# Splitting the last stage's weights during attention, 256 columns per pair, with both parts waiting in DRAM

## The reference

```python
xn = layernorm(x)
qu, ku, vu, qc, kc, vc = split(xn @ W_qkv.T)          # 8 heads of 64 each
term1     = causal(qc * s @ vu.T)                     # s = 64 ** -0.5
lookahead = causal(sigmoid(qu * s @ ku.T))
Su        = term1 @ lookahead.T
scores    = qc * s @ kc.T - silu(Su)                  # masked above the diagonal
attn_out  = (softmax(scores) @ vc) @ W_out.T
h         = silu(xn @ (w_gate / 127).T) * (xn @ (w_up / 127).T)
out       = x + attn_out + h @ (w_down / 127).T
```

## Time and profile before

| what | value |
|---|---|
| median of 3 runs | 1144.9 us |
| profiled execution, own time | 1145.91 us |
| profiled execution, span of its instructions | 1144.2 us |
| PE busy | 1092.3 us (95% of the span) |
| DVE, ACT, POOL busy | 815.2, 763.5, 534.2 us (71%, 67%, 47%) |
| DMA | 73.22 MB, mean 64 GB/s |
| mean granted TensorE clock | 0.988 of full |

### The profile page before, as it was taken

One profiled execution on the slowest core, in us unless ns is written; L12 is line 12 of the kernel. 1 busy time (PEld: TensorE's weight loads), 2 busy tenths in 40 slices (PEclk: granted clock), 3 DMA queues, 4 the chain that ended last, 5 costly groups with the idle time before them and its releaser, 6 DMA issues.

```text
span 1144.2 us, 21233 instructions
## 1 busy us (share of the span) xinstructions
PE 1092.3 (95%) x7936; PEld 992.5 (87%) x7936; DVE 815.2 (71%) x1671; ACT 763.5 (67%) x1371; POOL 534.2 (47%) x623
## 2 busy tenths in 40 slices
PE   5899999999999999999999999999999859999997
PEld 4799999999898899998999899999999757888997
DVE  5577677777777777777777777777667777567665
ACT  4577777777777777777777777777777846344333
POOL 0255556455645564555455555555555554231130
PEclk9999999999999999999999999999999969999999
DMA  8000201020002000200020012001100403745641
GB/s 284 1 2 19 75 22 22 17 77 22 22 17 76 24 25 13 80 21 20 17 76 20 19 24 70 20 19 39 37 20 19 157 19 130 274 149 176 224 152 57
DMA packets 36952, 73.22 MB, mean 64 GB/s; under 512 B 2288, under 2 KB 15856, under 8 KB 34800
## 3 DMA queue, kind: packets, MB, share of 16 engines
q1 hardware_dynamic: 36848, 71.84, 20.0%
HBM read 42.47 MB, written 32.24 MB: 65 GB/s over the span
## 4 chain that ended last, share of the span: by engine, by line
PE 87%; DVE 7%; issue 2%; ACT 1%; DMA 1%; DVEq 0%; POOL 0%; SPq 0%; ACTq 0%
PE X L637 23%; PE X L561 20%; PE X L675 8%; PE X L752 7%; PE X L743 6%; PE X L591 6%; PE X L646 6%; PE X L605 4%; PE X L576 4%; DVE prob L1147 3%; PE X L621 2%; DMA v_s<-heads_out 1%; PE X L552 1%; DVE low_max L1106 0%; DVE L_s L1200 0%
## 5 line engine op out<-in xcount | busy, mean ns | idle before, releaser
L637 PE MATMUL X<-L_s,T_s 128*128 128x128 f32 (+3 forms) x1920 | 278.9, 303 | 10.0 <-DVE L_s L1119 10.0
L487 POOL TENSOR_SCALAR prob<-prob,inv 128x512 f32<-128x512 f32 (+3 forms) x256 | 278.0, 1103 | 17.1 <-DVE inv L1159 17.1
L637 PEld LDWEIGHTS X<-L_s,T_s 128*128 128x128 f32 x1920 | 267.0, 191 | 20.5 <-issue 10.1
L561 PE MATMUL X<-xT,W 128*128 128x512 f32 x960 | 237.5, 400 | 8.5 <-DVE least L1147 7.0
L561 PEld LDWEIGHTS X<-xT,W 128*128 128x128 f32 x960 | 178.8, 191 | 50.4 <-DVE least L1147 9.7
L900 ACT ACTIVATE gate<-X 128x1024 f32<-128x1024 f32 (+1 forms) x96 | 84.8, 883 | 130.1 <-PE X L637 130.1
L1147 DVE CUSTOM_DVE_ANT_0 prob<-X,gate 128x512 f32<-128x512 f32 (+3 forms) x256 | 109.9, 485 | 73.8 <-PE X L621 73.7
L1133 DVE SCALAR_TENSOR_TENSOR gate<-gate,X 128x1024 f32<-128x1024 f32 (+1 forms) x96 | 99.6, 1038 | 77.9 <-ACT gate L900 77.9
L908 ACT ACTIVATE prob<-prob,least 128x512 f32<-128x512 f32 (+3 forms) x256 | 141.2, 562 | 8.5 <-DVE least L1147 8.5
L477 POOL TENSOR_SCALAR_AFFINE_SELECT T_s<-T_s 128x512 fp32r<-128x512 f32 x128 | 111.1, 889 | 67.0 <-DVE T_s L1126 67.0
L469 POOL TENSOR_SCALAR_AFFINE_SELECT tanh_l<-tanh_l 128x256 f32<-128x256 f32 (+1 forms) x96 | 46.2, 497 | 205.6 <-ACT tanh_l L878 205.6
(11 more groups left out here) (82 smaller groups left out, 1816.3 us busy)
## 6 DMA issues: line engine op xcount, KB each, us to landing
heads_out<-o_s SPq DMA_DIRECT2D x64, 256.0 KB, 3.3
xT_copy<-xT SPq DMA_DIRECT2D x8, 1024.0 KB, 7.6
xb<-in_L_attn_x SPq DMA_DIRECT2D x8, 512.0 KB, 5.8
xT<-xT_copy SPq DMA_DIRECT2D x4, 1024.0 KB, 5.2
tanh_l<-in_L_attn_x SPq DMA_DIRECT2D x8, 512.0 KB, 5.4
gate<-heads_out SPq DMA_DIRECT2D x4, 1024.0 KB, 8.0
T_s<-heads_out SPq DMA_DIRECT2D x4, 1024.0 KB, 9.7
L_s<-xT_copy SPq DMA_DIRECT2D x4, 1024.0 KB, 6.2
```

The source lines that it names most:

```text
L487: last = pool.tensor_scalar(v, v, inv[:, h, w - 1:w], None, ALU.mult)
L561: last = pe.matmul(out, sh.W[:, a, k, cols], xT[:, c, k, :], start=(n == 0), stop=(n == 3 * KD - 1))
L637: last = pe.matmul(both[:, h, at:at + (J + 1) * P], T_s[:, h, a, to:to + P], L_s[:, h, c, WIDE[J + 1]:WIDE[J + 1] + (J + 1) * P], start=(J ...
```

## The change

The four weights, 22 chunks of 128 x 256 (18 of integers, 4 of W_out), are now loaded, split and stored one chunk a step, in steps 4 to 25. SP's step stores the two parts of the last chunk and loads the next raw one; ACT copies a chunk to its high part; DVE subtracts and, for integer chunks, takes the largest low part. The flag is made piece by piece in steps 22 to 25. The DRAM tensors `w_split` hold both parts, so step 31 loads twice the bytes and splits nothing. The early DRAM copies are gone, and so is SP's wait for the maxima ahead of the load of the attention output. PE waits for the loads instead of the subtractions. In `ffn_first` ACT now does the second group of exp of pair 31 ahead of `copy_o`.

```diff
+CHUNK = 256
+INT_CHUNKS = 3 * KD * HIDDEN // CHUNK
+CHUNKS = INT_CHUNKS + OT * DIM // CHUNK
+FIRST_CHUNK = 4
...
             def step(part, b, q, g, back1, back2, ahead):     # SP
+                c = g - FIRST_CHUNK
+                if 1 <= c <= CHUNKS:
+                    store_chunk(c - 1)
+                if 0 <= c < CHUNKS:
+                    load_chunk(c)
+                if c == INT_CHUNKS + 1:
+                    sp.wait_ge(low_most_taken, 1)
+                    sp.dma_start(low_row[:, :], low_most[:, :]).then_inc(low_max_gathered, 16)
...
                     load_xT(0)
+                    sp.wait_ge(chunk_stored, CHUNKS * 16)
                     for n in range(4):
-                        sp.wait_ge(w_copied[n], 16)
-                        sp.dma_start(placed[n][:, LOW, :].bitcast(F32 if n == 3 else I32), w_copy[n]).then_inc(w_loaded[n], 16)
+                        sp.dma_start(placed[n].bitcast(F32), w_split[n]).then_inc(w_loaded[n], 16)
...
+            def load_chunk(c):
+                n, at = chunk_of(c)
+                src = (w_gate, w_up, w_down, W_out)[n]
+                r, d = at // src.shape[1] * P, at % src.shape[1]
+                to = w_raw[:, :].bitcast(F32) if n == 3 else w_raw[:, :]
+                sp.dma_start(to, src[r:r + P, d:d + CHUNK]).then_inc(chunk_loaded, 16)
+            def store_chunk(c):
+                n, at = chunk_of(c)
+                sp.wait_ge(w_low, c + 1)
+                sp.sem_inc(ticks, 1)
+                sp.dma_start(w_split[n][:, :, at:at + CHUNK], w_parts[:, :, :].bitcast(F32)).then_inc(chunk_stored, 16)
...
-            copy_weights()
...
             load_xres(0)
-            sp.wait_ge(low_max_taken, 3)
-            sp.dma_start(low_row[:, :], low_max[:, :]).then_inc(low_max_gathered, 16)
             sp.wait_ge(scores_emptied, after(LAST_G, 2))
             load_o(0)
...
             def ffn_first(products):                          # PE
-                pe.wait_ge(w_low, 2)
+                pe.wait_ge(w_loaded[0], 16)
+                pe.wait_ge(w_loaded[1], 16)
...
+            def high_chunk(c):                                # ACT
+                act.wait_ge(chunk_loaded, c * 16 + 16)
+                if c > 0:
+                    act.wait_ge(chunk_stored, c * 16)
+                raw = w_raw[:, :].bitcast(F32) if chunk_of(c)[0] == 3 else w_raw[:, :]
+                act.activation(w_parts[:, HIGH, :], raw, ACT.Copy).then_inc(w_high, 1)
...
                 exp_of(LAST_G, 0)
+                exp_of(LAST_G, 1)
                 copy_o(LAST_G - 1, double[3])
-                exp_of(LAST_G, 1)
...
+            def low_chunk(c):                                 # DVE
+                dve.wait_ge(w_high, c + 1)
+                raw = w_raw[:, :].bitcast(F32) if chunk_of(c)[0] == 3 else w_raw[:, :]
+                dve.tensor_tensor(w_parts[:, LOW, :], raw, w_parts[:, HIGH, :].bitcast(F32), ALU.subtract) \
+                   .then_inc(w_low, 1)
...
                 low_L(g, 2)
-                if part == LAST and q == 3:
-                    low_weights(2)
+                if 0 <= g - FIRST_CHUNK < CHUNKS:
+                    low_chunk(g - FIRST_CHUNK)
                 if ahead:
                     low_proj(g + 1, VU, par)
...
                     low_values(g + 2, (q + 1) // 2 % 2, (q + 1) % 2)
+                if 0 <= g - FIRST_CHUNK < INT_CHUNKS:
+                    take_low_max(g - FIRST_CHUNK)
```

More of the change, by code:

```diff
@@ L170, with layer @@
 BEFORE = bank_history()
-def layer(nc, x, W_qkv, w_gate, w_up, w_down, W_out, w_copy, xT_copy, sh, heads_out, out):
+def layer(nc, x, W_qkv, w_gate, w_up, w_down, W_out, w_split, xT_copy, sh, heads_out, out):
     ctx = ExitStack()
@@ L273, in layer @@
         w_loaded = [sem(f"w_loaded{i}") for i in range(4)]
-        w_copied = [sem(f"w_copied{i}") for i in range(4)]
+        chunk_loaded = sem("chunk_loaded")
+        chunk_stored = sem("chunk_stored")
         low_max_taken = sem("low_max_taken")
+        low_most_taken = sem("low_most_taken")
         low_max_gathered = sem("low_max_gathered")
@@ L1032, in step @@
                     exp_of(g - 1, 0)
-                if part == LAST and q == 3:
-                    high_weights(1)
                 if ahead:
@@ L1039, in step @@
                 high_L(g, 2)
-                if part == LAST and q == 3:
-                    high_weights(2)
                 if ahead:
@@ L1045, in step @@
                     high_xT(part, b)
-                if part == LAST and q == 3:
-                    high_weights(3)
                 if ahead:
@@ L1222, in ffn_first @@
                 minus_scores(LAST_G, 2, double[1])
-                take_has_low()
                 inverse(LAST_G, 1)
@@ L1296, in step @@
                     minus_scores(g - 1, 2)
-                if part == LAST and q == 3:
-                    low_weights(0)
                 if ahead:
                     low_proj(g + 1, QU, par)
-                if part == LAST and q == 3:
-                    low_weights(1)
-                if ahead:
                     low_proj(g + 1, KU, par)
@@ L1313, in step @@
                     ln.scale(dve, b + 1)
-                if part == LAST and q == 3:
-                    low_weights(3)
                 if ahead:
                     low_values(g + 2, (q + 1) // 2 % 2, (q + 1) % 2)
+                if 0 <= g - FIRST_CHUNK < INT_CHUNKS:
+                    take_low_max(g - FIRST_CHUNK)
+                if g - FIRST_CHUNK >= INT_CHUNKS:
+                    take_has_low(g - FIRST_CHUNK)
                 if back1:
@@ L1330, in step @@
                     low_PT(g - 1, 0)
-                if part == LAST and q == 3:
-                    take_low_max(0)
-                    take_low_max(1)
-                    take_low_max(2)
                 silu_of(g, 2)
@@ L1363, in build @@
         sh = Shared(nc, ctx)
-        layer(nc, x_rows, W_qkv, w_gate, w_up, w_down, W_out, w_copy, xT_copy, sh, heads_out, out_rows)
+        layer(nc, x_rows, W_qkv, w_gate, w_up, w_down, W_out, w_split, xT_copy, sh, heads_out, out_rows)
 _INS = ["L0_attn_x", "L0_attn_W_qkv", "L0_attn_W_out", "L0_ffn_w_gate", "L0_ffn_w_up", "L0_ffn_w_down"]
```

52 lines of the change are left out of this document (25 added, 27 removed).

## The result

The changed kernel takes **1133.6 us** (median of 6 runs, 1131.33 to 1135.83). The kernel before, run beside it, takes 1144.9 (6 runs, 1143.78 to 1145.54). The ratio is 0.9903, with a 95% interval of 0.9889 to 0.9916: about 1% faster. The forecast was 1132.7, range 1129.5 to 1137.5. The profiled execution was the slowest of the six: own time 1135.83, span 1134.0 us, against 1145.91 and 1144.2. Two single executions of about twice the usual time, one of the kernel before (2061 us, beside the runs on the chunks) and one of warm_start (2104 us), are left out of all that follows.

A forecast was written before the change was run, and what follows sets the result against it. The prediction took PE to set the pace, with two long idle waits around step 31. Its terms, 3.7 + 5.0 + 2.8 + 0.7 = 12.2 us, took the median of 1144.9 to 1132.7 us, range 1129.5 to 1137.5.

The forecast's parts named there:

- What bounds the kernel: Steady attention: PE sets the pace; around step 31 it idles 9.96 us ahead of `sum_up` and 6.18 ahead of `drain`.
- Term 1: Ahead of `sum_up` of step 31: splitting removed, PE's wait shrinks from 9.96 to 6.2 us, -3.7 us; clock still falls.
- Term 2: Ahead of `drain`: DVE's three reductions removed, PE's wait falls from 6.18 to 1.1 us, -5.0 us.
- Term 3: Scores and attend of `drain`: after a short wait the clock stays full, 4.96 us instead of 7.80, -2.8 us.
- Term 4: `ffn_first`: with ACT's exp done earlier, the third gate product comes 4.6 us after attend instead of 5.34, -0.7 us.
- Term 5: The 22 steps that get chunk work: hidden under idle time of ACT and DVE, 0 us; 27 us if none were hidden.
- Term 6: SP and DMA: the extra chunk transfers and step 31's doubled weight load stay hidden, the latter by 25 us; 0 us.
- The sum: Whole kernel: 3.7 + 5.0 + 2.8 + 0.7 = 12.2 us, all on PE's path, giving 1132.7 us.
- Rival A: Chunk steps: POOL's norm blocks DVE's subtractions, costing 2 to 6 us, 1135 to 1139 us; chance 0.10.
- Rival B: Last stage: POOL's additions slow DVE, PE waits, clock falls again, 4 to 5 us come back, 1137 us; chance 0.08.
- Rival C: Every chunk step: ACT or DVE late for `sum_up`, slower than before, up to 15 us over, 1160 us; chance 0.03.
- Rival D: Ahead of `drain`: ACT's gate, not DVE's reductions, set the wait; terms 2 and 3 nil, 1140.5 us; chance 0.05.

The follow-up runs named there:

- warm_start: Changed kernel plus unused matmuls and transposes in PE's waits at the start, meant to remove the start's scatter; 1135.5 us.
- subtract2: Changed kernel with two DVE operations of 128x1536 put back ahead of the last L_s of step 31, without ACT's copies; 1135.9 us.
- warm31: Changed kernel with 24 unused matmuls on PE in the 6.2 us wait ahead of `sum_up` of step 31; 1130.3 us.
- reduce3: Changed kernel with three reductions of 1536 columns put back on DVE ahead of the last gate of step 31; 1139.9 us.
- order_only: Kernel before with only ACT's order changed: second group of exp of pair 31 ahead of `copy_o`; 1144.5 us, ratio 0.9994.
- chunk3: Changed kernel with each chunk's copy, subtraction and reduction done three times, at the change's place; 1137.9 us.
- flag_late: Changed kernel with the last two flag operations moved back to `ffn_first`, behind the last row minima; 1137.1 us.
- chain1: Changed kernel with each chunk's copy and subtraction, once each, moved into the chain ahead of the step's last L_s; 1133.5 us.
- chain3: Changed kernel with chunk copy and subtraction moved ahead of the step's last L_s, and every chunk operation done three times; 1169.9 us, ratio 1.0198.
- reduce1: Changed kernel with one reduction of 1536 columns put back on DVE ahead of the last gate of step 31; 1137.8 us.
- again: The changed kernel itself, unedited, run and profiled once more; 1133.7 us.

## Why the prediction was right, step by step

- **What bounds the kernel** held: only the two long waits and what follows them moved, and steps 3 to 31 take as long as before to 0.2 us.
- **Term 1** was right to 0.05 us, with its reason: DVE's queue brings the wait back by itself (subtract2), and by the rows ACT's high part would have been next. That the clock would fall all the same was right too: 0.50 behind 6.21 us of waiting. The "up to 3 us more" of a clock that holds were 2.4 on the 48 matmuls, and 3.3 on the medians, when warm31 made it hold.
- **Term 2** was right to 0.02 us (reduce3 gives it back).
- **Term 3** was right in size (-3.08 against -2.8), and its cause was half of it. The prediction read the 7.80 us of `drain` as a slow clock alone. In that profile the clock was indeed low to the end of attend, but where it comes up sooner, the kernel before needs 7.81 all the same, for the flag (order_only), and only with the early flag 6.18 (reduce3). So by these two runs 1.5 of the 3.1 us come from the shorter wait, and the other 1.6 from the early flag. The right size was luck: it was read from one profile in which the clock stayed low for 6.4 us behind the restart, as long as the flag held PE. In order_only, behind the same wait, it was up after some 3 us and PE then stood idle for 1.51 us: a reader of that profile would have seen that the clock is only a part of the 7.80.
- **Term 4** was right on the timeline (4.77 us; forecast 4.6). Alone it brings 0.65 us on the timeline and between the medians, too little for the runs to show it (order_only).
- **Term 5**, 22 chunk steps at no cost, was right: 798.3 and 798.1 us, the same 28 waits of 6.4 us, and rows of 402, 412 and 407 ns (forecast 0.5, 0.4 and 0.35 us). The cover at q = 1 was said to be 1.2 us: one chunk fits, and with three of each PE waits 0.4 us in exactly these six steps (chunk3).
- **Term 6** was right on the weights, whose load ends about 913, 25 us before PE asks. But this is where the prediction has a hole: it named the flag nowhere as a cost, and the change makes it some 190 us early. That is worth 3.4 us with everything else in place (flag_late). The sum came out right because the flag's share stood in term 3 under the name of the clock, and that is luck.
- **The sum** of the terms was -12.4 against -12.2 forecast. The spans of the two profiles differ by 10.2, because this one began 1.7 us late for reasons of its own start, and lost 0.5 behind. On medians it is -11.3, and 0.9 over the forecast.
- **Rival A** (DVE held up by norm) falls: the 22 subtractions take 411 to 414 ns (at 296.2 in step 9 norm is on), and norm in step 9 takes 8.73 us (8.66 before). In chain1, where the subtraction follows ACT's copy at once, all 22 take 0.65 us, 0.24 more; norm is on in both places, so it is not norm alone, and the cause is open. **Rival B** (the gain given back in the last stage) was 0.5 us in the profile, a wait of 0.9 us there for L_s; warm_start is this rival in full. **Rival C** (slower) needs about three times the work in the chain: the point at which it decides was given as 0.55 us a step, and chain3 with 1.5 us comes out 23 us slower. **Rival D** falls by reduce3.

## What to carry to other kernels

Before you call a slow stretch "the clock", look for a second thing that ends at the same time: here a flag of 0.4 us of work, read 1.2 us later, lay exactly under a slow restart. A faster restart was worth nothing while the flag was late, and the early flag alone half of what both are worth. A wait of 3 us costs its length and half as much again for the restart, so the last 1 to 2 us of shortening count double; and where the wait can't go, matmuls that nobody needs can hold the clock. Work moved from a bare stage into a steady one costs nothing only where its engine is idle for an engine it doesn't feed: one chunk a step cost nothing that the runs show at either of two places, but three times that work cost 4 us at one of them and 36 at the other.

## What the runs showed of the hardware that was not expected

- **A short wait can be enough.** The granted clock went from 1.00 to 0.50 behind 2.87 us of idle TensorE (reduce1), and behind 2.07 us, some 1.1 us after PE had restarted (flag_late). It stayed at 1.00 behind 1.20 us (changed kernel) and 1.51 us (order_only). The restart of `drain` cost 1.5 us in reduce3 and reduce1 alike, for waits of 6.18 and 2.87 us; the clock stayed low for 3.1 to 3.5 us of work there and in order_only, and for 6.4 us in the profile before, behind the same 6.18.
- **PE reads a flag late.** From the end of DVE's flag to PE's first matmul: 1.16, 1.17 and 1.27 us in three profiles (before, order_only, flag_late). 0.49 us of it is the load of the flag (TENSOR_LOAD); the timeline of PE shows the wait as "issue" or not at all. In the first of the three attend ended at the same time, so only the other two measure it.
- **POOL is slower beside DVE's subtractions on the weights.** Norm of step 31, eight operations, took 12.98 us beside the subtractions on the weights, 10.70 beside subtract2's two operations (more than 11 was expected), and 8.50 in the changed kernel, without any:

```profile
915.68 10.70 POOL L518 TENSOR_SCALAR prob<-prob,inv 128x512 f32<-128x512 f32 x8
```

- **DVE can be held up, but by POOL's additions, not by norm.** DVE's L_s of 128x512 in the last stage takes 686 ns (median of 48) and up to 1786, beside POOL's additions of two SBUF tensors (1.78 and 0.68 us above). Beside norm, which reads one tensor, DVE's rows never showed a whole operation of waiting. The Trainium skill (SBUF — State Buffer, section "SBUF: two separate sides", on the ports that VectorE and GpSimd share) lets each of the two exclude the other; by these rows that holds for the additions, and for norm only in POOL's direction.
- **The start of an execution scatters.** Step 3 begins at 112.5 us before, 114.3 in the changed kernel, 111.6 in `again`: the granted clock in 32 to 36 and 56 to 60 us was between 0.50 and 1.00, for the same instructions.
